# Attention outputs computed in two column tiles of TensorE, with the group-norm sums, transposes and next normalisation rearranged around them

## The reference, cut to what matters

```python
h = concat([patch_embed(x), txt], axis=1)            # (8, 548, 192)
n = layernorm(h)
q, k, v = (n @ Wq.T, n @ Wk.T, n @ Wv.T)             # 3 heads of 64
s = q @ k.T / 8 * decay                              # decay = gamma**(m-l) for m >= l, else 0
o = softmax(s) @ v                                   # per head; masked scores are 0, not -inf
o = (o - mean_head) / sqrt(var_head + 1e-5)          # over all tokens of a head: group norm
h = h + (o * gn_w + gn_b) @ Wo.T
h = h + moe(layernorm(h))                            # 16 experts, top 8 of a softmax router, gelu
```

## Time and profile before

| what | value |
|---|---|
| three timed runs | 840.21 us median (836.47, 840.21, 840.67) |
| the profiled execution | 836.19 us, span 834.4 us |
| mean granted TensorE clock | 0.985 of full speed |
| busy: PE, PEld | 789.5 us (95%), 659.7 us (79%) |
| busy: DVE, ACT, POOL | 554.5 us (66%), 506.7 us (61%), 106.0 us (13%) |
| chain that ended last, by engine | PE 77%, ACT 7%, DVE 6%, POOL 3% |

### The profile page before, as it was taken

The page is one execution under the profiler, slowest core; times in us unless marked ns, Lnnn a source line. Parts: engine busy times, 40 slices in busy tenths (PEclk is TensorE's granted clock), DMA queues, the critical chain, the costliest instruction groups (busy, mean ns, idle before and its releaser), DMA issues.

```text
span 834.4 us, 13462 instructions
## 1 busy us (share of the span) xinstructions
PE 789.5 (95%) x4336; PEld 659.7 (79%) x4336; DVE 554.5 (66%) x1559; ACT 506.7 (61%) x1134; POOL 106.0 (13%) x187
## 2 busy tenths in 40 slices
PE   6698999999999898899999999999999999999997
PEld 2577778787787766778888888888888888888885
DVE  6567767768776767666666657666666576666654
ACT  1277877978778764565645646646556566464453
POOL 2130302203020229301001001010010010100000
PEclk9689999999999999999999999999999999999999
DMA  7400101011030216403324124223242342232410
GB/s 231 149 20 20 41 1 39 0 39 39 0 95 2 59 53 168 116 27 120 96 59 117 62 84 119 56 78 106 62 115 64 85 119 56 77 89 61 124 48 18
DMA packets 44380, 60.82 MB, mean 73 GB/s; under 512 B 4018, under 2 KB 37762, under 8 KB 44322
## 3 DMA queue, kind: packets, MB, share of 16 engines
q1 hardware_dynamic: 44322, 60.10, 25.5%
HBM read 52.04 MB, written 8.05 MB: 72 GB/s over the span
## 4 chain that ended last, share of the span: by engine, by line
PE 77%; ACT 7%; DVE 6%; issue 4%; POOL 3%; POOLq 1%; DVEq 1%; DMA 1%; SPq 0%; ACTq 0%
PE ps L1203 71%; ACT pr L614 4%; PE ps L1338 3%; DVE sc L923 1%; ACT v L532 1%; PE ps L1241 1%; DVE k_lo L884 1%; POOL w_lo L497 1%; PE ps L1392 1%; DMA gate<-comb_dram 1%; ACT ot L532 1%; ACT k_hi L532 1%; PE ps L1511 0%; PE ps L1512 0%; POOL w_r L495 0%
## 5 line engine op out<-in xcount | busy, mean ns | idle before, releaser
L1113 DVE TENSOR_TENSOR act<-act,gate 128x480 f32<-128x480 f32 (+1 forms) x216 | 144.6, 670 | 114.8 <-ACT act L731 108.5
L1203 PE MATMUL ps<-x,w_hi 128*128 128x480 f32 (+1 forms) x648 | 215.9, 387 | 0.0
L731 ACT ACTIVATE act<-ps 128x480 f32<-128x480 f32 (+1 forms) x216 | 124.0, 574 | 125.8 <-PE ps L1203 125.7
L1203 PE MATMUL ps<-x,w_lo 128*128 128x480 f32 (+1 forms) x432 | 164.7, 381 | 0.0
L884 DVE TENSOR_TENSOR act_lo<-act,act_hi 128x480 fp32r<-128x480 f32 (+1 forms) x216 | 145.6, 674 | 0.2
L1203 PEld LDWEIGHTS ps<-x,w_hi 128*128 128x128 f32 x648 | 121.6, 188 | 19.6 <-ACT act L731 0.2
L532 ACT ACTIVATE act_hi<-act 128x480 fp32r<-128x480 f32 (+1 forms) x216 | 130.7, 605 | 6.8 <-DVE act L1113 6.8
L1203 PE MATMUL ps<-pt,v 68*128 68x512 f32 (+5 forms) x288 | 85.6, 448 | 7.9 <-DVE gvar L974 7.9
L1203 PEld LDWEIGHTS ps<-x,w_lo 128*128 128x128 f32 x432 | 81.2, 188 | 13.1
L1203 PE MATMUL ps<-act_hi,w_hi 128*128 128x480 f32 (+1 forms) x216 | 83.9, 388 | 4.5 <-DVE act_lo L884 4.5
L1203 PE MATMUL ps<-act_lo,w_hi 128*128 128x480 f32 (+1 forms) x216 | 83.4, 386 | 0.0
(11 more groups left out here) (173 smaller groups left out, 1259.7 us busy)
## 6 DMA issues: line engine op xcount, KB each, us to landing
gate<-comb_dram SPq DMA_DIRECT2D x112, 240.0 KB, 3.2
gate<-comb_dram SPq DMA_DIRECT2D x32, 256.0 KB, 4.0
w_raw<-w SPq DMA_DIRECT2D x16, 384.0 KB, 3.8
h_dram<-h SPq DMA_DIRECT2D x8, 384.0 KB
res<-h_dram SPq DMA_DIRECT2D x7, 360.0 KB, 4.4
out<-res SPq DMA_DIRECT2D x7, 360.0 KB, 3.2
h<-txt SPq DMA_DIRECT2D x3, 672.0 KB
decay_rows<-drow SPq DMA_DIRECT2D x1, 1014.0 KB, 8.7
```

Source lines behind the costliest of these rows:

```text
L731: a.activation(act[j % 3][:, 0:n], ps[:, up_bank(j), 0:n], ACT.Gelu_apprx_tanh).then_inc(gelu_done, 1)
L1113: dve.tensor_tensor(act[j % 3][:, 0:n], act[j % 3][:, 0:n], gate[e % 4][:, 0:n], ALU.mult).then_inc(gated, 1)
L1203: return pe.matmul(dst, w, x, start=start, stop=stop)
```

## The change

**In the matmuls.** `attend` writes two column tiles: the output of query tiles 0, 3, 4 goes to partitions 0 to 63 of one bank, that of tiles 1, 2 to partitions 64 to 127 of the same bank, each with the head's own 64 columns of v as weights. Every head has a bank of its own (6, 7, 2). `v` has no padding, so `V_W` is 192 and `v_copy` has one copy for each bank; `pt` is laid out in the order in which the two tiles read it. `o_copy` runs for every head: two copies for heads 0 and 1, four for head 2. On the host, the doubled last 64 columns of Wv go.

**In the order.** Transposes group 1 of head 2 stands behind the k of head 2, group 3 goes to bank 7; `gn_sums` writes bank 1 and stands, with the wait for its bank, ahead of `attend(b, 0)`; the wait for the variance stands behind the first transposes of head 1. `gn_variance` on VectorE stands behind `normalise(b, 1)`. GpSimd normalises the next batch's tokens (`norm_next`) instead of ScalarE, and token tile 1 of the expert part (`norm_second`) in the last body; VectorE's `second_norm(0)` stands behind the last part of `qk_rest`, its `second_norm(1)` in the last body. The hardware loop is written out.

```diff
-QK_W, V_W, O_W, R_W = 512, 256, D, E
+QK_W, V_W, O_W, R_W = 512, D, D, E
-PT_BANKS = [(0, 1, 3, 0), (0, 1, 3, 0), (2, 3, 2, 3)]
+PT_BANKS = [(0, 1, 3, 0), (0, 1, 3, 0), (2, 3, 2, 7)]
+ATTEND_TILES = ((0, 3, 4), (1, 2))
+ATTEND_W = (2 * P + LAST, 2 * P)
+PT_AT = {4: 0, 2: L, 3: L + 3 * P, 1: L + 7 * P, 0: L + 9 * P}
...
-            body(0, tail=False, later=False, more=True, ahead=True)
-            body(1, tail=True, later=False, more=True, ahead=True)
-            with eng.Fori(2, B - 2) as b:
-                body(b, tail=True, later=True, more=True, ahead=True)
...
+            for b in range(B):
+                body(b, tail=b > 0, later=b > 1, more=b < B - 1, ahead=b < B - 2)
...
+            def norm_next(b):
+                pool.drain()
+                pool.wait_ge(xt_done, nth(b - 1, 2, 2))
+                apart(pool, "pool")
+                for I in range(NT):
+                    r = rows(I)
+                    pool.tensor_scalar(xn[:r, I, 0:D], tokens(h, b, I), rstd[:r, I:I + 1], nmr[:r, I:I + 1], ALU.mult, ALU.add)
+                pool.drain()
+                pool.tensor_copy(xn[:, :, D:256], xn[:, :, P:D]).then_inc(xn_ready, 1)
...
                 if more:
                     rstd_of(b + 1, ln1_var, rstd, mv, veps, nmr, ln1_rstd)
+                    norm_next(b + 1)
                 halve_w1(b)
                 if tail:
                     gn_coefficients(b - 1)
-                if more:
-                    twice(ln1_normed, nth(b, 1, 1), xn, xn_ready)
+                if not more:
+                    second_rstd(1)
+                    pool.drain()
+                    pool.wait_ge(x2t_done, 2)
+                    norm_second()
...
-                    copy(v[:r, t0:t0 + n, 0:HD], src[:, :, 0:HD])
-                    copy(v[:r, t0:t0 + n, P + HD:3 * P], src[:, :, HD:256]).then_inc(v_copied, 1)
+                    copy(v[:r, t0:t0 + n, :], src[:, :, 0:D]).then_inc(v_copied, 1)
...
+                at = 0
+                for half, n in enumerate(ATTEND_W):
+                    for p in ((0,), (HD,), (0, HD))[hh]:
+                        last = copy(ot[p:p + HD, hh // 2, at:at + n], ps[HD * half:HD * half + HD, bank, 0:n])
+                    at += n
...
                 pt_copy(b, 0)
-                if more:
-                    norm_apply(b + 1, rstd, nmr, ln1_rstd, xn, ln1_normed)
-                else:
+                if not more:
                     logits_exp(0)
                 if tail:
                     y_round(t, 0)
...
                 exps(b, 2, (0,))
-                o_copy(b, 0)
+                o_copy(b, 0, 6)
+                o_copy(b, 1, 7)
...
                 normalise(b, 0)
                 if tail:
                     gn_partial(t)
+                normalise(b, 1)
+                if tail:
                     gn_variance(t)
                 if not more:
-                    router_shift(0, 7)
-                normalise(b, 1)
-                if not more:
+                    router_shift(0, GN_BANK)
+                    second_norm(1)
                     router_top(0)
...
+            def attend(b, hh, bank):
+                c = slice(hh * HD, hh * HD + HD)
+                for J, copied in ((4, 2), (2, 2), (3, 3), (1, 4), (0, 4)):
+                    pe.wait_ge(pt_copied, nth(b, 4 * H, 4 * hh + copied))
+                    k, at = (KEY_LAST if J == NT - 1 else P), PT_AT[J]
+                    for half, tiles in enumerate(ATTEND_TILES):
+                        n = sum(rows(I) for I in tiles if I <= J)
+                        if n:
+                            out_ = ps[HD * half:HD * half + HD, bank, 0:n]
+                            last = mm(out_, v[:k, J, c], pt[:k, at:at + n], J == NT - 1, J == half)
+                            at += n
+                last.then_inc(o_done, 1)
...
                 qk(b, tail, later, (0, 1, 2))
                 if tail:
-                    probs_transpose(t, 2, (0, 1))
+                    probs_transpose(t, 2, (0,))
                 qk(b, tail, later, (3,))
                 if tail:
-                    pe.wait_ge(pt_copied, nth(t, 4 * H, 2 * 4 + 2))
+                    probs_transpose(t, 2, (1,))
+                    pe.wait_ge(pt_copied, nth(t, 4 * H, 2 * 4 + 1))
                     probs_transpose(t, 2, (2, 3))
...
                 pe.wait_ge(pt_copied, nth(b, 4 * H, 1))
                 probs_transpose(b, 0, (3,))
+                pe.wait_ge(pt_copied, nth(b, 4 * H, 2))
                 if not more:
-                    logits(0, 7)
+                    logits(0, GN_BANK)
                 if tail:
                     gn_sums(t)
+                attend(b, 0, 6)
+                pe.wait_ge(pt_copied, nth(b, 4 * H, 4))
+                probs_transpose(b, 1, (0,))
                 if tail:
                     pe.wait_ge(gn_var, nth(t, 1, 1))
                 if not more:
                     pe.wait_ge(l_sub, 1)
-                attend(b, 0)
-                pe.wait_ge(pt_copied, nth(b, 4 * H, 4))
-                probs_transpose(b, 1, (0, 1, 2))
+                probs_transpose(b, 1, (1, 2))
```

153 lines of the change are left out of this document (68 added, 85 removed).

## The result

The changed kernel takes 847.81 us (median, 845.89 to 848.35) beside 839.39 (836.42 to 840.67) for the kernel before on the same chip: a ratio of 1.0107, 95% interval 1.0083 to 1.0130. It is slower by 1.1%. The forecast was 834.0 and the range ended at 843. The sign is that of the two slower rivals, but neither of their mechanisms made it, as the experiments show.

A forecast was written before the change was run, and what follows sets the result against it. It took the 34.03 us batch loop as the bound, mostly TensorE's work with ScalarE close behind. Full-clock savings of -9.8 and +6.0 for the clock gave -3.8: 836.19 to 832.4, plus 1.6 for the median, 834.0; range 825 to 843.

The forecast's parts named there:

- the two slower rivals: Low clock lasts twice as long: 843.7, chance 0.13. A weight load per head's extra ones isn't hidden: 844.8, chance 0.07.
- VectorE beside GpSimd: GpSimd's normalisation, moved beside VectorE's head 2 division, slows VectorE by 0 to 1.2 us a batch; 0.1 taken.
- The outputs ... +1.2.: ScalarE's output copies: 0.6 us for each of heads 0 and 1, 1.2 for head 2; +1.2 a batch.
- The variance late: Group norm's variance behind head 1's division on VectorE: ScalarE idle 3.3 us, TensorE waiting 2.2 to 2.3, batch about 33.4.
- I take 1.94: Attend in two overlapping column tiles takes 1.94 us instead of 3.34, saving 1.40 a head.
- The drain on a change of mode: TensorE's array changes shape five more times a batch, at 0.1 us each, 0.5 a batch.
- The gain of the column tiles is real and lies off the loop that sets the period.: TensorE's work falls from 32.3 to 27.9 us a batch; almost all of the 4.35 turns into waiting.
- The clock, "+6.0": TensorE's new 2.2 us wait lowers its clock, costing 1.0 us a batch for six batches, +6.0.
- The first batch: First batch, without group norm and set by TensorE: two attends, narrower values and normalisations off ScalarE, less shape changes, -3.0 us.
- The seventh distance -1.3: Seventh distance between batches' first scores falls from 34.7 to 33.4 us, as second_norm(0) stands behind k.
- the first token tile: Expert part's first token tile: one shorter attend, -1.4 us; second_rstd(1) leaves the w2 split, removing a TensorE stop, -1.0.

The follow-up runs named there:

- e1: The changed kernel with the next batch's normalisation back on ScalarE, behind its copies of head 0's transposes: 841.21 us, 1.0030 to the kernel before.
- e2: The changed kernel with GpSimd's normalisation of the next batch put last in the batch, behind the group norm's coefficients: 841.78 us, 1.0040 to the kernel before.
- e10: e8 with head 2's second copy of the outputs made by VectorE from the first, except in the last batch: 830.48 us, 0.9922 to the kernel before.
- e4: The changed kernel with head 0's attend issued twice, the first result thrown away: 851.38 us, 1.0170 to the kernel before.
- e8: e2 with the variance ahead of head 1's division on VectorE: 840.00 us, 1.0019 to the kernel before.
- e9: e2 with head 0's attend issued twice: 841.08 us, 1.0022 to the kernel before.
- e3: The changed kernel with all four ScalarE copies of head 1's transposes ahead of the y operations: 846.72 us, 1.0116 to the kernel before.
- e12: e10 with the last batch's second_norm on VectorE in its old places and every attend issued twice: 841.11 us, 1.0049 to the kernel before.
- e6: The kernel before with normalisations on GpSimd ahead of the w1 split and the batch loop written out, no column tiles: 844.06 us, 1.0072 to the kernel before.

## Why the prediction was wrong

**VectorE beside GpSimd, "between nothing and 1.2 a batch; I take 0.1".** This step failed, and it is the largest single term. It does not decide the sign by itself: e1 and e2, without it, are still slower than the kernel before. It is 1.1 in the divisions (0.78 to 1.88) or 1.3 in the denominators (0.47 from the first addition to the reciprocal in e2, 1.75 in batch 4), near the upper end. The reason that I gave, "ScalarE's scaling is all that waits there", was wrong twice: TensorE waits 1.01 for just that scaling, and VectorE's own q_lo, q and k_lo stand behind the divisions. The prediction knew that the split would come 3.5 us later, and didn't put the new times of the two engines side by side: the split from S+26.6 to S+29.7 in batch 4, VectorE's denominators at S+28.1. It also priced only the long operations; the short ones stretch too. e1 and e2 give the price as about 6 us in all, of the 13.8 between forecast and median.

**"The outputs ... +1.2."** It priced the copies of 64 partitions and 292 or 256 columns at 0.3 each. They take 0.40 each, four in 1.60. Their lengths are those of the rule that it had read (0.16 and 0.84 ns a column), but they start 0.41 apart, so the overlap of 0.10 that it took off each is not there. The worse mistake is the place: head 2's four stand ahead of head 1's exponentials, so "S+11.4" was S+12.24 (the last of them ends at 157.08), and the v copies moved with them, which is the wait of 1.27. e10, which takes half of head 2's copies away, gains 0.94 a batch.

**The variance late.** Its place in the chain, and both its waits, were right: y at S+17.2 for S+16.7, ScalarE idle for 2.96 (3.3 forecast), TensorE for 2.33 (2.2 to 2.3). The division took 1.5, not 1.84; in the kernel before it had GpSimd's coefficients beside it, and here it has nothing of GpSimd's (head 0's, with nothing beside it, takes 1.57 in both). From the y to the last exponential the list took 11.0 for the forecast 10.0: 0.4 more of output copies, and 0.59 of waiting for the x's. So S+28.2 for 26.7.

The batch then adds up: 0.5 late at the y, 1.05 in ScalarE's list, 0.9 from the last exponential to the next S (7.6 for 6.7, the collision), together 2.4 on the forecast 33.4, measured 35.8 in batch 3. In batch 4 the last exponential ends at S+27.6, and 8.1 follow it.

**The attend, "I take 1.94".** Right, and a little better: 1.72 from start to start. The Trainium skill ("TensorE: Matmul & The Clock Gate", Part 3) says that loads without a change of row group don't overlap; 18 loads in 1.72 us left no room for exposed ones, so the trace goes against it here. The drain on a change of mode that the Trainium skill names ("TensorEngine Tiling (Array Packing)", Key Properties) is no more than the 0.1 taken: the step from the last scores into the attend takes 0.20 between starts, the step between the last two groups of scores 0.11.

**"The gain of the column tiles is real and lies off the loop that sets the period."** Right: in e4's profiled execution another attend doesn't lengthen an undisturbed batch.

**The clock, "+6.0".** Wrong in the other direction. It fell in every second batch, three times in six, and cost 0.4 at most. Batch 3 is 0.1 longer than the undisturbed ones (35.82 beside 35.71 and 35.74). Batch 5 (36.06) is 0.33 longer, but has another wait of 0.33 for the maxima, which e4's batch 5 has without a fall. Batch 1 (36.14) is 0.4 longer; in e2, e8 and e9 batch 1 is 0.33 longer than the shortest without a fall. The stretch of batch 3, with the columns of the windows view:

```profile
165.40:168.80 3.40, 3.40 (x19) 2.25 (x16) 1.62 (x9) 3.35 (x9) 1.55 (x3) 0.50 0.00 0
```

TensorE loses 0.9 at attend of head 1 (3.16 long for 2.28 in batch 4). ScalarE sets the pace, so its last exponential is only 0.6 late (S+28.2 for S+27.6), and the stretch behind it, where the collision has another victim, is 0.5 shorter (7.6 for 8.1). With about the same pause in e3, at another place, the clock stayed low for up to three times as long, and a batch lost up to 3.3. Without this term the forecast would have been 9.8 below the kernel before; the measured span without the falls in these batches is still over 11 above. The two errors had opposite signs, and the forecast looked better than its working.

**The first batch, "TensorE sets it ... -3.0".** It came to -0.25. (Two attends, the values and four changes of shape make -2.55 by its own prices; the rest was put on the normalisations without a price.) The waits of TensorE in it were one of 1.1 for the maxima before; they are 2.7 for the maxima, 0.9 for q and 0.8 for head 2's probabilities now. With the collision out (e2) it is -1.6. VectorE sets it in part; e4 and e12 show that TensorE's work counts there too.

**"The seventh distance -1.3"** was -0.17, and **the first token tile "-1.4 -1.0"** with the rest of the expert part +1.9. The stop of 1.43 at 339.48 did shrink, but TensorE's waits for act_lo up to the w2 split's end are now 0.87, 1.16, 1.18, 0.42 and 0.94, in sum 4.6, where they were 0.87, 1.02, 0.80 and 1.43, in sum 4.1. I had traced one stop to one GpSimd operation; they are a budget of VectorE's.

**The rivals.** The slower cases carried 0.20 and had the clock and the weight loads as their mechanisms. The largest real one, VectorE's contention, stood in the text as a term of 0.1 with a bound of 1.2 and had no case of its own. The six stretches that it touches (batches 0 to 5) at 1.1 for 0.1 would have brought the forecast to 840; the rest is ScalarE's longer list, the first batch and the expert part.

## What to carry to other kernels

When work moves to GpSimd, write the new times of its whole queue beside VectorE's, and price each overlap of operations that work from on-chip memory by the worst row; the short operations stretch as well; ask both who reads the slowed result and who stands behind it. When an engine's saving is forecast to turn into waiting, the next engine's list decides, and its copies cost by their columns, however few the partitions: two of head 2's four copies moved (e10) brought 0.94 a batch, and the three halved attends 0.77 (e12). Then repeat the saved work on purpose: e4 and e12 showed, with one line each, what the saving was worth in either kernel.

## What the runs showed of the hardware

- VectorE's divisions of head 2 (three operations from on-chip memory to on-chip memory) take 0.78 us alone and 1.88 to 1.89 beside GpSimd's two-operand splits, in the changed kernel and in e6, and two additions of five columns 0.71 and 0.89 for 0.17. In batch 6 of the changed kernel, which has no split, they are at 0.78 and 0.17. GpSimd's own splits hardly change (2.00 and 1.97 without, 2.06 and 2.08 with it). By what path the one slows the other no run shows.
- Float32 column tiles of 64 columns run beside each other: 18 instructions and 1,060 columns on the longer side in 1.72 us, 1.62 ns a column, where the full array took 1.83.
- A stretch of 3.4 us at the low clock (0.50) cost a batch 0.1 us in the changed kernel, where TensorE had waits to lose behind it. In e3, with 10.2 us at the low clock, a batch was 3.3 us longer.
- ScalarE's four copies of 64 partitions and 292 or 256 columns take 0.40 and 0.38 us and start 0.41 apart; they don't overlap.
- TensorE's pace in a loop without waits differs between kernels with the same matmuls there: 55.52, 55.71 and 55.83 us a token tile. The last came when two unused tiles moved the data (on another chip); the cause is open.
